# State recurrence over the chunks by doubling, with the powers of mu from GpSimd, and two copies of ends moved ahead of the last normalisation

## What is computed

```python
h = einsum('bfh,kh->bfk', frames(x), dct)          # 32 rows x 938 frames x 128
h = h + ssm(layernorm(h))                          # long convolution over the frames:
#   lambda = exp(-exp(nu) + i theta),  kernel[t] = gamma * lambda**t,  y = Re(kernel * x)
h = h + moe(layernorm(h))                          # 8 experts, each takes its 1024 best frames
```

## Time and profile before

| | us |
|---|---|
| runs of the kernel | 706.83, 709.85, 715.07; median 709.85 |
| the profiled execution | 711.25, of which the span of the core is 709.1 |
| front of half 0, with setup | 0 to 82 |
| ends, states, products of half 0 | 81 to 140 |
| second layer norm of half 0, front of half 1 | 140 to 252 |
| ends, states, products of half 1 | 252 to 312 |
| the rest: layer norm, router, experts | 312 to 709 |
| DVE busy / PE busy / ACT busy / POOL busy | 487 / 407 / 267 / 309 |

### The profile page before, as it was taken

The page is one execution under the profiler, slowest core; times in us unless marked ns, Lnnn a source line. Parts: engine busy times, 40 slices in busy tenths (PEclk is TensorE's granted clock), DMA queues, the critical chain, the costliest instruction groups (busy, mean ns, idle before and its releaser), DMA issues. The chain is left out here.

```text
span 709.1 us, 11791 instructions
## 1 busy us (share of the span) xinstructions
PE 407.4 (57%) x3448; PEld 321.7 (45%) x3448; DVE 487.0 (69%) x1848; ACT 266.6 (38%) x511; POOL 309.1 (44%) x207
## 2 busy tenths in 40 slices
PE   3877567789778657778610000024498899986000
PEld 3866456755677547755400000012366567665000
DVE  6798787686589978578788888879965766651000
ACT  4677500044567730015534355000263566551000
POOL 0555500054366630015610000007777888888875
PEclk9999889966999969998955555555598999999555
DMA  8799128898187705998521000001123244443332
GB/s 143 123 247 231 38 57 170 188 231 247 36 140 127 143 6 120 170 266 241 141 81 30 0 0 0 1 28 46 51 54 83 67 61 61 62 61 30 30 30 26
DMA packets 102063, 68.55 MB, mean 97 GB/s; under 512 B 8256, under 2 KB 99008, under 8 KB 102015
## 3 DMA queue, kind: packets, MB, share of 16 engines
q1 hardware_dynamic: 90750, 59.56, 37.7%
q0 software_dynamic: 11264, 8.40, 8.9%
HBM read 42.89 MB, written 24.03 MB: 94 GB/s over the span
## 5 line engine op out<-in xcount | busy, mean ns | idle before, releaser
L1450 POOL DMA_INDIRECT hid<-out,index x64 | 62.6, 978 | 131.9 <-DVE index L1318 114.0
L1467 POOL DMA_INDIRECT out<-hid,index x64 | 101.1, 1580 | 27.6 <-issue 19.8
L1438 POOL TENSOR_TENSOR small<-small,powers 120x16 f32<-120x16 f32 x16 | 46.4, 2900 | 151.8 <-DVE small L1031 151.8
L1007 DVE BATCH_NORM_STATS2 stats<-hid 120x6 f32 (+1 forms) x512 | 105.1, 276 | 9.3 <-ACT hid L570 8.4
L651 ACT ACTIVATE xt<-banks 128x480 f32<-128x480 f32 x64 | 36.4, 571 | 134.4 <-PE banks L814 134.4
L794 PE MATMUL banks<-xn,ring 122*120 122x128 f32 x512 | 69.9, 297 | 26.2 <-DMA xn<-s 10.8
L729 PE MATMUL banks<-const,xt 128*120 128x128 f32 x512 | 71.7, 287 | 15.9 <-ACT xt L565 15.9
L794 PEld LDWEIGHTS banks<-xn,ring 122*120 122x120 f32 x512 | 65.3, 206 | 30.9 <-issue 19.9
L1423 POOL TENSOR_TENSOR small<-small,powers 120x16 f32<-120x16 f32 x16 | 46.9, 2931 | 66.0 <-DVE small L1031 66.0
L729 PEld LDWEIGHTS banks<-const,xt 128*120 128x120 f32 x512 | 63.2, 190 | 21.8 <-ACT xt L565 14.0
L936 PE MATMUL banks<-w_ring,xn 128*128 128x128 f32 x512 | 62.8, 284 | 7.0 <-DVE hid L1377 7.0
(11 more groups left out here) (190 smaller groups left out, 719.8 us busy)
## 6 DMA issues: line engine op xcount, KB each, us to landing
ring<-toeplitz SPq DMA_DIRECT2D x128, 120.0 KB
xin<-in_x SPq DMA_DIRECT2D x14, 960.0 KB, 8.2
out<-hid SPq DMA_DIRECT2D x14, 960.0 KB, 11.4
w_ring<-in_L_ffn_W SPq DMA_DIRECT2D x16, 256.0 KB, 3.4
toeplitz<-ring SPq DMA_DIRECT2D x6, 545.0 KB, 9.2
out<-hid SPq DMA_DIRECT2D x2, 784.0 KB
xin<-in_x SPq DMA_DIRECT2D x2, 768.0 KB, 7.2
hid<-out,index POOLq DMA_INDIRECT x64, 2.6
```

Source lines behind the costliest of these rows:

```text
L1007: ins = dve.bn_stats(stats[:, slot, b, :], hid[:, bass.ds(c * HB + b, 1), :].rearrange("p a k -> p (a k)"))
L1438: pool.tensor_tensor(small[:, slot, 4, :], small[:, slot, 2, :], powers[0:L, :], ALU.pow).then_inc(rstd2_ready, 1)
L1450: pool.indirect_dma_start(found[:, n, :], None, rows, bass.IndirectOffsetOnAxis(ap=index[:, n:n + 1], axis=0)).then_inc(found_in[e % 2], 16)
L1467: pool.indirect_dma_start(rows, bass.IndirectOffsetOnAxis(ap=index[:, n:n + 1], axis=0), adds[:, n, :], None, compute_op=ALU.add, oob_is_e ...
```

## The change

The recurrence is solved by doubling. With E_c the end of chunk c, the program forms P_c = E_c + mu E_(c-1), then F_c = P_c + mu^2 P_(c-2), then S = F_c + mu^4 F_(c-4), each for all chunks at once, with zeros where an index would fall before the first chunk. mu^2 and mu^4 are computed by POOL once, between its constants and its first front chunk. `e2`, `pairs_of` and `fours_of` have zeros ahead of the first chunk; the last two lie in one buffer with the scratch of POOL's normalisation (`centre`) and with `wide`, so DVE clears their zeros again in each half. ACT copies the tiles r = 0 and 1 of the ends before its last normalisation, and the other six after it. SP moves 112 of the 128 columns of the ends (the last chunk has no use).

```diff
-        mu = sb("mu", [P, 3])
+        mu = sb("mu", [P, 3, 3])
+        mu_parts = sb("mu_parts", [P, 4])
-        centre = sb("centre", [L, HB - ACT_END, D])
+        between = sb("between", [P, 768])
+        centre = between[0:L, 0:(HB - ACT_END) * D].rearrange("p (b k) -> p b k", k=D)
+        pairs_of = between[:, 0:2 * 9 * HB].rearrange("p (r n) -> p r n", r=2)
+        fours_of = between[:, 2 * 9 * HB:2 * 20 * HB].rearrange("p (r n) -> p r n", r=2)
-        wide = sb("wide", [L, 2, HB, E])
+        wide = between[0:L, 512:768].rearrange("p (s b e) -> p s b e", s=2, e=E)
...
-                        sp.dma_start(e2[first:end, ri, :],
-                                     ends[ri:97 + ri:32, first // 16:end // 16]).then_inc(e_moved[g], 16)
+                        sp.dma_start(e2[first:end, ri, HB:COLS],
+                                     ends[ri:97 + ri:32, first // 16:end // 16, :, 0:COLS - HB]).then_inc(e_moved[g], 16)
...
-                    sp.wait_ge(s_ready, 3 * h + g + 1)
+                    sp.wait_ge(s_ready, 2 * (3 * h + g + 1))
...
-                normalise(CHUNKS - 1, 1, DVE_TILES, ACT_END)
                 for r in range(8):
                     act.wait_ge(e_ready, 8 * h + r + 1)
                     act.activation(ends[0:98, r], banks[0:98, 6 + r % 2, :].rearrange("p (a b) -> p a b", a=4),
                                    ACT.Copy).then_inc(e_copied, 1)
+                    if r == 1:
+                        normalise(CHUNKS - 1, 1, DVE_TILES, ACT_END)
...
+                def doubled(part, level, far_back, near, dst, done, count):
+                    dve.scalar_tensor_tensor(dst, far_back, mu[part, level, 0:1], near,
+                                             ALU.mult, ALU.add).then_inc(dve_own, own.one())
+                    dve.wait_ge(dve_own, own.all())
+                    for ri in range(2):
+                        m = (2, 1)[ri]
+                        dve.scalar_tensor_tensor(dst[:, ri], far_back[:, 1 - ri], mu[part, level, m:m + 1], dst[:, ri],
+                                                 ALU.mult, ALU.add).then_inc(done, count())
...
-                    for ri in range(2):
-                        dve.tensor_copy(state(ri, 1), end(ri, 0)).then_inc(dve_own, own.one())
-                    for c in range(2, CHUNKS):
...
-                    dve.wait_ge(dve_own, own.all())
-                    dve.nop().then_inc(s_ready, 1)
+                    doubled(part, 0, ends_of[:, :, 0:reach], ends_of[:, :, HB:HB + reach],
+                            pairs[:, :, 2 * HB:2 * HB + reach], dve_own, own.one)
                     dve.wait_ge(dve_own, own.all())
+                    doubled(part, 1, pairs[:, :, 0:reach], pairs[:, :, 2 * HB:2 * HB + reach],
+                            fours[:, :, 4 * HB:4 * HB + reach], dve_own, own.one)
+                    dve.wait_ge(dve_own, own.all())
+                    doubled(part, 2, fours[:, :, 0:reach], fours[:, :, 4 * HB:4 * HB + reach],
+                            sums[:, :, HB:HB + reach], s_ready, lambda: 1)
...
+                if h == 0:
+                    dve.wait_ge(powers_of_mu, 10)
+                dve.wait_ge(xn_pool, CHUNKS * (h + 1))
+                dve.memset(pairs_of[:, :, 0:2 * HB], 0.0).then_inc(dve_own, own.one())
+                dve.memset(fours_of[:, :, 0:4 * HB], 0.0).then_inc(dve_own, own.one())
+                dve.wait_ge(dve_own, own.all())
...
+            pool.wait_ge(mu_ready, 3)
+            for level in range(2):
+                if level:
+                    pool.wait_ge(powers_of_mu, 5)
+                real = mu[:, level, 0:1]
+                pool.tensor_tensor(mu_parts[:, 0:2], mu[:, level, 0:2], mu[:, level, 0:2],
+                                   ALU.mult).then_inc(powers_of_mu, 1)
+                pool.tensor_tensor(mu_parts[:, 2:4], mu[:, level, 1:3], real.broadcast_to([P, 2]),
+                                   ALU.mult).then_inc(powers_of_mu, 1)
+                pool.wait_ge(powers_of_mu, 5 * level + 2)
+                pool.tensor_tensor(mu[:, level + 1, 0:1], mu_parts[:, 0:1], mu_parts[:, 1:2],
+                                   ALU.subtract).then_inc(powers_of_mu, 1)
+                pool.tensor_tensor(mu[:, level + 1, 1:3], mu_parts[:, 2:4], mu_parts[:, 2:4],
+                                   ALU.add).then_inc(powers_of_mu, 2)
```

More of the change, by code:

```diff
@@ L211, in build @@
         s2 = sb("s2", [P, 2, COLS])
-        carry = sb("carry", [P, 2, HB])
         w1_ring = sb("w1_ring", [P, 2, F])
@@ L324, in build @@
         s_ready = sem("s_ready")
+        mu_ready = sem("mu_ready")
+        powers_of_mu = sem("powers_of_mu")
         y_ready = sem("y_ready")
@@ L944, in _ @@
             dve.memset(s2[:, :, 0:HB], 0.0)
+            dve.memset(e2[:, :, 0:HB], 0.0)
             dve.wait_ge(wr_sum, 1)
@@ L977, in _ @@
             dve.wait_ge(tables_ready, 2)
-            dve.tensor_copy(mu[:, 0:1], ANG[:, L:L + 1]).then_inc(dve_own, own.one())
-            dve.tensor_copy(mu[:, 1:2], RED[:, L:L + 1]).then_inc(dve_own, own.one())
-            dve.tensor_scalar(mu[:, 2:3], RED[:, L:L + 1], -1.0, None, ALU.mult).then_inc(dve_own, own.one())
+            dve.tensor_copy(mu[:, 0, 0:1], ANG[:, L:L + 1]).then_inc(mu_ready, 1)
+            dve.tensor_copy(mu[:, 0, 1:2], RED[:, L:L + 1]).then_inc(mu_ready, 1)
+            dve.tensor_scalar(mu[:, 0, 2:3], RED[:, L:L + 1], -1.0, None, ALU.mult).then_inc(mu_ready, 1)
             N1 = L + 1
@@ L1080, in _ @@
                 normalise(CHUNKS - 1, 1, 0, DVE_TILES)
+                def doubled(part, level, far_back, near, dst, done, count):
[6 more added lines that the diff above has]
+                                                 ALU.mult, ALU.add).then_inc(done, count())
                 def states(g):
                     part = slice(*GROUPS[g])
[L1086 to L1090, removed]
+                    ends_of, pairs, fours, sums = e2[part], pairs_of[part], fours_of[part], s2[part]
+                    reach = COLS - HB
                     if due(32 * h):
@@ L1094, in states @@
                     dve.wait_ge(e_moved[g], 32 * (h + 1))
-                    for ri in range(2):
-                        dve.tensor_copy(state(ri, 1), end(ri, 0)).then_inc(dve_own, own.one())
-                    for c in range(2, CHUNKS):
-                        dve.wait_ge(dve_own, own.all())
-                        for ri in range(2):
-                            dve.scalar_tensor_tensor(carry[part, ri, :], state(0, c - 1), mu[part, ri:ri + 1],
-                                                     end(ri, c - 1), ALU.mult, ALU.add).then_inc(dve_own, own.one())
-                        dve.wait_ge(dve_own, own.all())
-                        for ri in range(2):
-                            m = (2, 0)[ri]
-                            dve.scalar_tensor_tensor(state(ri, c), state(1, c - 1), mu[part, m:m + 1],
-                                                     carry[part, ri, :], ALU.mult, ALU.add).then_inc(dve_own, own.one())
-                    dve.wait_ge(dve_own, own.all())
-                    dve.nop().then_inc(s_ready, 1)
+                    doubled(part, 0, ends_of[:, :, 0:reach], ends_of[:, :, HB:HB + reach],
+                            pairs[:, :, 2 * HB:2 * HB + reach], dve_own, own.one)
+                    dve.wait_ge(dve_own, own.all())
+                    doubled(part, 1, pairs[:, :, 0:reach], pairs[:, :, 2 * HB:2 * HB + reach],
[3 more added lines that the diff above has]
+                            sums[:, :, HB:HB + reach], s_ready, lambda: 1)
                 def add_products(i):
```

## The result

| | before | after |
|---|---|---|
| median, us (4 runs each) | 708.64 | 695.73 |
| lowest to highest | 706.83 to 715.07 | 694.37 to 697.49 |
| profiled execution / its span | 711.25 / 709.1 | 694.37 / 692.4 |

The ratio is 0.984 with a 95% interval of 0.980 to 0.987, and 0.982 (0.980 to 0.985) in a second comparison on another chip: 11.5 to 12.6 us gained. The medians differ by 12.9 us; they count every execution, the ratios leave out those that fell into a slower state of the chip. The forecast was 699.5 us, a range of 694.5 to 706, and a gain of 11 us. The whole interval lies beyond the 1% that it took as distinguishable from no change.

A forecast was written before the change was run, and what follows sets the result against it. The stage was taken as bound by the start of PE's products and the issue of group 2's states. 4.8 + 4.6 us plus 1.6 us of clock gave 11.0 us: 700.3 by the profiled execution, 698.9 by the median, taken as 699.5, range 694.5 to 706.

The forecast's parts named there:

- The chain up to the products: Ends to PE's products: ends 1.05 us earlier in half 0, group 0's states 2.8 us, PE's start 93.6 not 96.44.
- The recurrence: DVE's states: 3.4 us for group 0, not 5.17, and 3.5 us for group 2, not 5.4.
- The memsets: Two DVE memsets of some 0.15 us each end before the ends arrive, 0.35 us to spare: no cost.
- POOL: Eight small operations before its first reciprocal root, at most 9.4 us against 8.5 us of slack; first pow still at 22.1.
- Rival (d): POOL's small operations cost as much as its pow, 2.93 us; above 2.4 us each the kernel is at 715; chance 0.04.
- fill(1): SP's refill of the ring waits for the first two products and starts at 97.4 instead of 101.03, 3.6 us earlier.
- The clock: PE may stay at full clock through products(0), up to 1.7 us more per half; 1.6 us taken of 0 to 3.4.
- Group 2's issue as the gate: SP's issue of group 2's states decides what follows: 4.8 us earlier in half 0, 4.6 in half 1, 9.4 together.
- Rival (b): SP's fills of the ring decide, only fill(1)'s earlier start counts: 7.2 us gained, 703.4; chance 0.14.
- Rival (a): Ends in 448-byte rows reach DVE late, some 1.2 us more as a bound: 6.2 us gained, 704.5; chance 0.16.
- The size: Whole kernel: 9.4 us from both halves plus 1.6 us of clock, 11.0 us gained, 699.5 us.

The follow-up runs named there:

- warm_pe: Changed kernel plus twelve 128x128 matmuls on PE in its pause between the ends and the products; ratio 0.981 (0.979 to 0.984).
- old_group2: Changed kernel with group 2 alone using the recurrence of the kernel before; ratio 0.990 (0.987 to 0.993).
- group2_early: Changed kernel with group 2's states computed before the first adds and sent between fill(1) of slots 0 and 1; ratio 0.985 (0.983 to 0.987).
- rows_512: Changed kernel with the ends moved in rows of 512 bytes again, all 128 columns; ratio 0.988 (0.985 to 0.990).
- two rings: Changed kernel with a second equal ring in memory of input frames and copied ends for i = 1 and 3, fills written out; ratio 0.986 (0.983 to 0.989).
- the spare ring: Changed kernel with a second ring, in memory of input frames and copied ends, for i = 2 alone, fills written out; ratio 0.986 (0.983 to 0.989).

## Why the prediction was right, and where not

**The chain up to the products** came out to 0.2 us: ends 0.87 us earlier (1.05), states of group 0 at 2.8 us (2.8), PE's start at 2.9 us (2.8).

**The recurrence** was priced from 16 and 121 columns at 3.4 and 3.5 us and takes 3.23 and 3.32. From the changed kernel, DVE's groups by shape:

```profile
L1094 DVE SCALAR_TENSOR_TENSOR between<-e,mu,between 32x112 f32<-32x112 f32 x4 | 1.1, 320 | 0.1
...
L1089 DVE SCALAR_TENSOR_TENSOR between<-e,mu 32x224 f32<-32x224 f32 x2 | 0.9, 442 | 0.7 <-DMA e<-xin 0.6
```

The forecast had 335 and 469 ns. The formula of the Trainium skill (VectorE: DVE Perf Modes, the TRN2 errata), which it states for an fp32 tensor_tensor add, gives 274 and 391 ns, some 50 ns too little for this form. The step from 112 to 224 columns, 122 ns, is 1.09 ns a column, close to the formula's 1.04. The two operations of a pair overlap, 0.57 us for two of 0.32. The Trainium skill (VectorE: DVE Perf Modes, the section on the DRAIN) says that the next op does not start until the pipeline is empty, and that one which is not held starts earlier; the pairs agree with that exception.

**The memsets** end at 85.42, ahead of 86.06: covered, as said.

**POOL** needed 1.7 us for the powers:

```profile
13.48 0.19 POOL L1431 TENSOR_TENSOR mu_parts<-mu 128x2 f32<-128x2 f32 x1 [12.60 <-DVE mu L985]
...
15.01 0.20 POOL L1438 TENSOR_TENSOR mu<-mu_parts 128x2 f32<-128x2 f32 x1
23.65 2.93 POOL L1447 TENSOR_TENSOR small<-small,powers 120x16 f32<-120x16 f32 x1 [8.44 <-DVE small L1036]
```

Eight operations of about 0.2 us, then 8.4 us of waiting. Rival (d) is out. The first pow did not stay at 22.1, but what it waits for there is DVE's moments, not POOL.

**fill(1)** started 4.6 and 4.0 us earlier and not 3.6. In the kernel before it waited for no product: it started right behind SP's last issue of group 2's ends (the first row below, to set beside fill(1) at 101.03 in the earlier trace rows), so SP's own queue behind group 1's states held it. In the changed kernel that queue is free at 94.96 and fill(1) starts at 95.21, when PE has the second product.

```profile
99.74 1.25 SPq L487 DMA_DIRECT2D e<-xin  x2
```

```profile
93.71 1.25 SPq L492 DMA_DIRECT2D e<-xin  x2
```

The forecast put the second product 3.8 us behind PE's start, at the low clock. It came 2.9 and 3.5 us behind it. In half 0 the first product still ran at full clock (its add comes 1.2 us behind PE's start), because the clock falls inside the window 92 to 94.

**The clock** is the term that was mis-sized. The forecast read its falls in the kernel before at 93.9 and 267.9; the windows' 0.93 and 0.95 give 93.7 and 267.8. It counted 1.6 us for a PE that stays at the full clock through products(0). The clock fell there in both halves of the changed kernel too. The eighth add ended 9.7 and 9.5 us behind PE's start where it was 10.0 and 9.6 before: 0.3 and 0.1 us, 0.4 in all. Even a warm PE would not have given the 1.7 us a half that stood as the upper end, since warm_pe shows SP's queue letting through only 0.8 and 0.4.

**Group 2's issue as the gate.** 5.3 and 4.9 us were measured where 4.8 and 4.6 stood; the term's sign and size hold. Of half 0's 5.3 us, 2.9 come from PE's earlier start, 0.3 from the faster adds and 2.1 from the recurrence of group 2. That it is the gate is half right. In the kernel before SP stood still for it, 2.25 us in half 0 and 1.3 in half 1, and old_group2 shows that a late group 2 would hold the stage again. With the change SP stands still 1.1 us in half 0 and not at all in half 1 (it finishes fill(1) at 267.10 and issues at 267.15). From there an earlier group 2 is worth nothing, as group2_early shows, and in the two traces of the kernel before a shift of 0.5 to 0.7 us didn't move the stage end either. Whether fill(1)'s start takes over is not shown: the time from it to the stage end was 36.6 to 38.1 us in the changed kernel's two traces, 36.4 to 37.9 with whole rows, with group 2 early and with a warm PE, and 40.0 in half 0 with the fills written out.

**Rival (b)**, the ring holding the gain back, is where the changed kernel has arrived, but it did not hold this gain back: the stage end moved by more than fill(1)'s start (5.2 and 6.5 us against 4.6 and 4.0). **Rival (a)** is out by rows_512; its bound of 1.2 us did not follow from the 3.0 and 2.7 us that it named. **The size**: 11.7 us from the stages against 11.0, and this closeness is in part luck. At group 2's issue the two halves had gained 10.2 us, where the forecast had 11.0 with its clock term. The rest comes from behind the issue, which the forecast took as fixed: 27.8 and 28.6 us became 28.0 and 27.0. In half 1 of the kernel before, the clock was low there from 284.9 to 288.3 us; in half 1 of the changed kernel it stayed full. That is a likely cause of the 1.6 us, not a shown one.

**Why filling faster didn't help.** The traces of the ring kernels show it in good part. A slot is 488 KB, which takes 2.3 us at 218 GB/s, and PE needs 2.04 us for the two products of a slot. Over the last seven slots PE began a pair every 2.5 and 2.4 us in the changed kernel and every 2.3 and 2.7 us with two rings; with the spare ring it was 2.7 and 2.6, and in the kernel before 2.5 and 2.6. With two rings SP had issued its last slot 3.7 and 2.6 us earlier, but PE began its last pair 0.6 us earlier in half 0 and 2.8 us later in half 1. One window each from this part of half 0, of the changed kernel, with two rings, and with the fills written out:

```profile
116.00:126.00 10.00, 8.16 (x67) 1.00 0.73 192
```

```profile
117.00:127.00 10.00, 8.33 (x66) 1.00 1.07 220
```

```profile
118.00:128.00 10.00, 7.53 (x63) 1.00 1.07 199
```

The changed kernel leaves the transfers a share of 0.73, and 192 GB/s come of it; without SP's pauses the share is full, and 199 to 220 GB/s come of it. PE gets no more done. SP's loop, at 2.55 us a slot, already asks for about what the transfers deliver, and slots issued faster wait longer for their data. Earlier fills also let the loads behind them in SP's queue start earlier, and these share the transfers with the last slots: two loads of 960 KB of frames from 127.55 us on in half 0 with the fills written out, the experts' vectors and weights from 287.90 us on in half 1 with two rings. These are two of the late stage ends, 55.62 and 55.72 us; how much of them is due to this no run separates.

**What stays open** is how much sooner the ring could be ahead when this last part begins. Every ring kernel keeps group 2's states between fill(1) and fill(2), and none combines an early group 2 with a second ring.

## What to carry to other kernels

Replace a chain of many small dependent vector operations by fewer wide ones when the fixed cost is most of each: twelve pairs on 16 columns took 5.2 us, three levels on 112 and 224 columns 3.2 us. Follow the saving through the queue that carries it: it counts up to the next thing in that queue that is late, so look for how long the queue stands still there (2.25 and 1.3 us before, 1.1 and nothing after) before spending more on the same gate. More room for transfers helps only while their rate isn't the limit: compare the time of a slot's bytes at the rate of the trace with the time of the work on it. And take the moments relative to the stage's own start when two executions differ by a clock that falls somewhere else.

## What the runs showed of the hardware

- The granted clock fell to 0.5 in the second layer norm of half 0 for anything from nothing to over 20 us in executions of nearly the same kernel. The stretch that holds it took 107.0 us with none and 112.4 us with 24.
- Twelve matmuls of 128x128 in a pause of 3.5 us kept the granted clock full, where without them it fell within 1 us of the start of the next work.
- SP issued a slot's five transfers in 2.05 us where they are written out and in 2.55 us inside its loop. Either way PE got a slot of 488 KB every 2.3 to 2.8 us at the end of the stage: at a DMA share of 0.73 they moved 192 GB/s, at 1.07 they moved 199 and 220.
- Vector operations with a scalar per partition took, on 32 partitions, 320 ns on 112 and 442 ns on 224 columns; two that don't wait for each other took 0.57 us together and not 0.64.
- GpSimd's multiply on two columns took 0.2 us, its pow on 16 columns 2.9 us.
